# Scoring an attention in both orientations: keys on the partitions instead of transposed probabilities, in five attentions of a four-level decoder on one core

## What is computed

```python
s = q @ k.T * D ** -0.5          # 128 queries x nk keys
s = where(causal, s, -inf)       # L0_attn and L2_attn only
a = softmax(s, axis=-1)
o = a @ v
out = x + concat(o) @ Wo (+ bo)
```

## Time and profile before

| | |
|---|---|
| median of 3 runs | 4947.15 us (4937.4 to 4949.03) |
| profiled execution: span from its first to its last instruction | 4969.4 us |
| profiled execution: own time beside the span | none is given; the span stands 22.2 us above the median of the runs |
| PE busy | 4410.3 us, 89% |
| DVE busy | 2640.3 us, 53% |
| ACT busy | 2593.2 us, 52% |
| POOL busy | 836.2 us, 17% |
| mean granted TensorE clock | 0.958 |

### The profile page before, as it was taken

The page is one execution under the profiler, slowest core; times in us unless marked ns, Lnnn a source line. Parts: engine busy times, 40 slices in busy tenths (PEclk is TensorE's granted clock), DMA queues, the critical chain, the costliest instruction groups (busy, mean ns, idle before and its releaser), DMA issues.

```text
span 4969.4 us, 84778 instructions
## 1 busy us (share of the span) xinstructions
PE 4410.3 (89%) x29077; PEld 2535.4 (51%) x29077; DVE 2640.3 (53%) x6880; ACT 2593.2 (52%) x9813; POOL 836.2 (17%) x1454
## 2 busy tenths in 40 slices
PE   7888989989999999989799888998889888898796
PEld 3544764444454454448355444454455454554493
DVE  5555225655655655645454656556664565546523
ACT  4556434454454454453555556555655566555542
POOL 0111420011011011035021021110131021210350
PEclk9999989999999999999899989999999999999897
DMA  5000540000000000007000000000000000000172
GB/s 198 11 11 11 172 128 18 12 7 28 12 7 28 12 7 18 6 22 222 22 22 10 5 5 24 14 10 1 6 23 14 9 6 10 10 1 1 46 230 76
DMA packets 107750, 183.05 MB, mean 37 GB/s; under 512 B 13344, under 2 KB 69408, under 8 KB 107200
## 3 DMA queue, kind: packets, MB, share of 16 engines
q1 hardware_dynamic: 92544, 147.48, 9.9%
q0 software_dynamic: 13632, 28.04, 1.6%
q10 hardware_dynamic: 1152, 2.10, 0.1%
HBM read 126.33 MB, written 51.23 MB: 36 GB/s over the span
## 4 chain that ended last, share of the span: by engine, by line
PE 65%; DVE 20%; ACT 7%; issue 5%; DMA 2%; POOL 1%; SPq 0%; DVEq 0%; POOLq 0%; ACTq 0%
PE bank L713 8%; PE bank L866 7%; PE bank L883 6%; DVE rowmax L1693 6%; PE bank L745 4%; PE bank L1041 3%; PE bank L733 3%; PE bank L1152 3%; PE bank L1141 3%; PE bank L1023 3%; PE bank L790 3%; DVE probsT L1759 2%; PE bank L922 2%; PE bank L852 2%; ACT work L1323 2%
## 5 line engine op out<-in xcount | busy, mean ns | idle before, releaser
L1323 ACT ACTIVATE work<-bank,rowmax 128x128 f32<-128x128 f32 (+1 forms) x3072 | 1061.1, 398 | 208.6 <-DVE rowmax L1693 208.6
L1693 DVE TENSOR_REDUCE rowmax<-bank 128x4 f32<-128x512 f32 (+2 forms) x1152 | 614.0, 578 | 433.4 <-PE bank L866 314.8
L713 PE MATMUL bank<-mask_causal,identb 128*128 128x512 bf16 x2839 | 803.1, 394 | 22.6 <-DVE qd L1628 8.7
L883 PE MATMUL bank<-ident,work 128*128 128x128 f32 (+1 forms) x4096 | 641.0, 282 | 155.6 <-DVE probsT L1759 116.7
L1323 ACT ACTIVATION_READ_ACCUMULATOR work<-bank,rowmax 128x1 f32 x3072 | 753.1, 245 | 0.0
L883 PEld LDWEIGHTS bank<-ident,work 128*128 128x128 f32 (+1 forms) x4096 | 481.8, 144 | 377.7 <-DVE probsT L1759 196.8
L1759 DVE COPY probsT<-bank 128x512 f32<-128x512 f32 (+2 forms) x832 | 482.0, 601 | 55.3 <-PE bank L883 53.9
L713 PEld LDWEIGHTS bank<-mask_causal,identb 128*128 128x128 bf16 x2839 | 273.5, 101 | 290.7 <-issue 115.5
L866 PE MATMUL bank<-km,q 32*128 32x512 f32 (+2 forms) x1792 | 403.7, 562 | 1.9 <-issue 1.9
L2206 POOL TENSOR_TENSOR qd<-work 128x256 f32<-128x256 f32 (+1 forms) x64 | 64.7, 1012 | 1902.9 <-ACT work L1321 1836.5
L1257 ACT ACTIVATE part<-bank,eps 128x512 f32<-128x512 f32 x232 | 157.7, 680 | 383.8 <-PE bank L745 383.3
(11 more groups left out here) (336 smaller groups left out, 6902.5 us busy)
## 6 DMA issues: line engine op xcount, KB each, us to landing
slot<-in_w_L_ffn SPq DMA_DIRECT2D x78, 578.0 KB
slot<-in_w_stream SPq DMA_DIRECT2D x41, 512.0 KB
expert_rows<-slot SPq DMA_DIRECT2D x36, 516.0 KB, 6.3
slot<-in_w_L_ffn SPq DMA_DIRECT2D x39, 450.0 KB
qd<-expert_rows SPq DMA_DIRECT2D x117, 129.0 KB
back<-pair_rows SPq DMA_DIRECT2D x24, 512.0 KB, 5.3
slot<-in_w_stream SPq DMA_DIRECT2D x16, 256.0 KB
pair_rows<-qd,dest POOLq DMA_INDIRECT x234
```

The source lines that it names most:

```text
L713: nc.tensor.matmul(b[:], identb[:], mask["causal"][:].unsqueeze(1).to_broadcast([P, 4, P]), start=True, stop=True)
L883: ins = nc.tensor.transpose(b[0:nk, j * P:(j + 1) * P], probs[t % 2][:, r, j, 0:nk], ident[:])
L1323: ins = nc.scalar.activation(out, raw, ACT.Exp, bias=top, accum_out=expsum[t % 2][:, 4 * r + j:4 * r + j + 1])
L1693: V.tensor_reduce(m[:, 4 * r:4 * r + J], banks.where(("scores", n, c, s, r))[:, 0:J * nk] .rearrange("p (j k) -> p j k", j=J), AX_X, ALU.m ...
```

## The change

Five attentions get a body of their own, `keyed_mha`. The scores are made twice. The first time, with queries on the partitions, they only give the maxima. The second time, with the keys on the partitions (weights: the keys of one head; moving: its queries), they are what the exponential reads, so its result is already `probsT` and no transpose follows. Per item and engine:

- PE: `half(t, rows)` interleaves the score matmuls of two row groups of item t with the keyed ones of the two other row groups of item t-1, so that all four row tiles have work. Masked attentions add the mask to both, the second time with the mask as weights and the identity as moving operand. `turn_tops` turns the maxima (bf16, as value and remainder) with one matmul, `shift` adds them to the keyed scores with sixteen small bf16 matmuls (`top_pick`, 32 rows, as weights), `totals` makes the sums over the keys with sixteen matmuls on four column tiles, already spread over the features, `attend` and `output` are as before. The fillers in the body are gone but for six at t = 0 and four at t = 1.
- ACT: one copy of the turned maxima to bf16, four exponentials of 512 columns without bias and accumulator, Ln and Exp (scale -1) of the sums.
- DVE: the four maxima as before, two small instructions that split them in value and remainder (`split_tops`), `context`. No reciprocal, no copies out of PSUM.
- POOL: nothing (the halving sums of the three unmasked ones are gone).
- Rings: scores and turned maxima in banks 0 to 2, keyed scores and projections in 3 to 5, attend in 6, totals in 7.

Around it, `average64` gives way to a corner of `average` with a scale in the Ln, `after_mask` becomes bf16, `xcol` moves into `lcol`.

```diff
+KEYED = ("L0_attn", "L1_xattn", "L2_attn", "L2_a2", "L3_ffn",)
+FRONT_ROWS, BACK_ROWS = (0, 1), (2, 3)
...
-                             "head": (4, 5)})
+                             "head": (4, 5), "first": (0, 1, 2), "second": (3, 4, 5)})
...
+            return not st["linear"] and not st["mask"] and not keyed(st) and r in POOL_SUMS
...
+                    def half(t, rows):
+                        back = BACK_ROWS if rows == FRONT_ROWS else FRONT_ROWS
...
+                            for r in rows:
+                                b = bank(("scores", n, c, s, r), ("row_max", (n, c, s, r)), "first")
+                                if st["mask"]:
+                                    nc.tensor.matmul(b[:, 0:4 * nk], identb[:], mask[st["mask"]][:].unsqueeze(1)
+                                                     .to_broadcast([P, 4, P]), start=True, stop=False)
+                        if 1 <= t <= GROUP:
+                            c, s = items[t - 1]
+                            for r in back:
+                                b = bank(("keyed", n, c, s, r), ("probsT", (n, c, s, r)), "second")
+                                if st["mask"]:
+                                    nc.tensor.matmul(b[:], mask[st["mask"]][:], identb[:].unsqueeze(1)
+                                                     .to_broadcast([P, 4, P]), start=True, stop=False, skip_group_check=True)
+                        for j in range(4):
...
+                                    elif j == 0:
+                                        nc.tensor.matmul(b[:, 0:4 * nk], B["q"][c][g32, s * P:(s + 1) * P],
+                                                         km[c][g32, s, :, 0:nk], start=not st["mask"], stop=True
...
+                                    if D == 32:
+                                        keys, queries = k4[c][g32, j, s * nk:(s + 1) * nk], q4[c][g32, j, s * P:(s + 1) * P]
+                                    else:
+                                        keys, queries = km[c][g32, s, j, 0:nk], B["q"][c][g32, s * P:(s + 1) * P]
+                                    nc.tensor.matmul(banks.where(("keyed", n, c, s, r))[0:nk, j * P:(j + 1) * P], keys, queries,
+                                                     start=j == 0 and not st["mask"], stop=False, skip_group_check=True)
...
+                    def turn_tops(t):
...
+                        pe.wait_ge(*have("tops", (n, c, s)))
+                        nc.tensor.matmul(b[:, 0:P], tops[:], identb[:], start=True, stop=True
...
+                    def shift(t, rows):
...
+                        if rows == BACK_ROWS:
+                            pe.wait_ge(*have("tops_taken", (n, c, s)))
+                        for j in range(4):
+                            for r in rows:
+                                g32 = slice(32 * r, 32 * r + 32)
+                                ins = nc.tensor.matmul(banks.where(("keyed", n, c, s, r))[0:nk, j * P:(j + 1) * P],
+                                                       top_pick[g32, j:j + 1].to_broadcast([32, nk]), topsT[g32, :], start=False, stop=True,
+                                                       skip_group_check=True)
...
+                    def totals(t):
...
+                                if D == 32:
+                                    ins = nc.tensor.matmul(b[g32, j * P:(j + 1) * P], average[0:nk, 0:32], probsT[t % 2][0:nk, r, j, :],
+                                                           start=True, stop=True)
+                                else:
+                                    ins = nc.tensor.matmul(b[g32, 0:P], W("head_ones", nk)[:, 24 - 8 * j:56 - 8 * j],
+                                                           probsT[t % 2][0:nk, r, j, :], start=j == 0, stop=j == 3)
...
+                    for t in range(GROUP + 2):
+                        if t == GROUP + 1:
+                            step(then)
+                        if t == 0:
+                            warm(6, "second")
+                        half(t, FRONT_ROWS)
+                        if 1 <= t <= GROUP:
+                            turn_tops(t - 1)
+                        if t >= 2:
+                            totals(t - 2)
+                        elif t == 1:
+                            warm(4, "second")
+                        if 1 <= t <= GROUP:
+                            shift(t - 1, BACK_ROWS)
+                        half(t, BACK_ROWS)
+                        if 1 <= t <= GROUP:
+                            shift(t - 1, FRONT_ROWS)
...
+                        if t >= 2:
+                            attend(t - 2)
+                        if t == GROUP + 1:
+                            step(then)
+                        for c in C:
+                            if t == output_step(c):
+                                output(c)
...
+                    def soften(t):
...
+                        for r in BACK_ROWS + FRONT_ROWS:
+                            act.wait_ge(*have("keyed", (n, c, s, r)))
+                            nc.scalar.activation(probsT[t % 2][0:nk, r, :, :], banks.where(("keyed", n, c, s, r))[0:nk, :]
+                                                 .rearrange("p (j t) -> p j t", j=4),
+                                                 ACT.Exp).then_inc(*made("probsT", (n, c, s, r)))
+
+                    def invert(t):
...
+                        nc.scalar.activation(out, banks.where(("summed", n, c, s))[:, 0:w * P].rearrange("p (i t) -> p i t", i=w),
+                                             ACT.Ln, scale=float(P) if D == 32 else 1.0).then_inc(*made("log_sum", (n, c, s)))
+                        act.wait_ge(*have("log_sum", (n, c, s)))
+                        nc.scalar.activation(out, out, ACT.Exp, scale=-1.0).then_inc(*made("inverse", (n, c, s)))
```

239 lines of the change are left out of this document (231 added, 8 removed).

## The result

The forecast was wrong, in sign too. The changed kernel takes 5155.99 us (median of 4 runs, 5113.23 to 5178.47), the kernel before 4948.09 beside it (4 runs, 4937.4 to 4954.45): **1.0405 times as long, 95% interval 1.0346 to 1.0464**. Forecast were 4902 us and a range of 4850 to 4990. The profiled execution of the change took 5171.79 us with a span of 5170.1, which is 200.7 more than the span before.

The account below looks back on a forecast made before the run. PE was taken as the bound after the change, ACT's bound in masked items gone. Changes of -5.5, +1.6, -4.7, -1.7 and -1.0 us per body, four bodies each, gave -45 us from 4947: 4902 us, range 4850 to 4990.

Parts of the forecast that it names:

- The likeliest case: Whole kernel: new bodies save 45 us, 4902 us; with its better neighbour, the wait mostly covered (4855), chance 0.60.
- the clock: Rival: without fillers PE's granted clock drops, 7 us more low level in each of 20 bodies, 4972 us; chance 0.08.
- the forecast's own rule: Clock rival's pricing: half of the added low-level time is lost, +70 us over the 20 bodies.
- the forecast of -45: All five attentions, four bodies each: change against the kernel before, 45 us less.
- Items at 2.4 GHz: Time per item inside the bodies: masked 7.07, L3_ffn 5.79, 77 keys 5.85 us.
- last intervals: End of a body, up to the last attend: 2.5 us, 3.0 where a matmul centres the next norm.
- The wait for the exponential: Unmasked items' back half: PE waits for ACT to free a keyed bank, 0.95 us after the first shift.
- The passes do not queue up: Likeliest case: four tiles run at once, 1.08 us per half; opposite rival, queueing: +110 us, 5012, chance 0.12.
- the shift's weights are fast: Likeliest case: an item's two shifts cost 0.25 and 0.32 us; opposite rival, slow weights: +49 us, 4951, chance 0.20.
- The starts of bodies: Time to first attend: 16.0 us in L3_ffn, 14.3 L1_xattn, 23.0 L2_a2, 18.9 L2_attn, 22.6 L0_attn.
- The routing term: Masked bodies: routing matmuls of the group before add 1.2 us per body.
- the -11 of the masked bodies: Four bodies each of L0_attn and L2_attn: forecast change of -6.8 and -4.0 us.

Follow-up runs that it names:

- e14_first_item_fill: Change in three unmasked attentions only, banks recut, six fillers at each body's head and four at its first turn: 4867.31 us, 0.9824 of the kernel before.
- e11_rings_head_fill: Change in three unmasked attentions only, banks recut, six fillers at each body's head and two in each item: 4912.84 us, 0.9915 of the kernel before.
- e4_xattn_only: The change in L1_xattn alone, the other four attentions as in the kernel before: 5107.68 us, 1.0196 of the kernel before.

## Why the prediction was wrong

- **The likeliest case failed at one step: the clock, priced at 7 us of low level per body with a chance of 0.08.** The reason written against it was "a stall is under 1 us and followed by dense work". The stalls were of that size, 0.63 and 0.77 with one of 1.25. What failed is the second half: in bodies with 77 keys the dense work of the items did not bring the clock back in any of the 33 bodies that were low there, even with PE busy for 36 of 36 us. The low time was 294 us in four bodies of L1_xattn and 188 in four of L2_a2, 60 us per body and not 7. The mechanism was on the list; its size was off by a factor of over eight in these two kinds, and its chance was far too low. Over all twenty bodies the low time grew by 535 us and not by 140. By the forecast's own rule, that half of it is lost, that is an estimated 267 us, which covers the 246 between the forecast of -45 and the measured +201.
- **I took it as one price for all bodies.** L3_ffn has 128 keys and got 7 to 14 us of low level per body; there the clock does come back within the body, and the price of 7 was about right.
- **Items at 2.4 GHz were right.** Masked 7.05 (forecast 7.07), L3_ffn 5.85 (5.79), 77 keys 5.74 (5.85), last intervals 2.28 to 2.31 and 2.96 (2.5 and 3.0), end 2.9 (3.0). The wait for the exponential is there, 0.77 to 0.84 per unmasked item (0.95; the 0.69 in it came from a row of the norm's Ln, and the 512-wide exponentials, L1487, took 0.59 in the mean), ACT's busy time in an L0_attn body fell to 26.5 us (some 30), and the variance matmul waits for the square (34 times, 23.9 us in all). Bodies that kept the clock, with fillers in that wait: 57.8, 55.6, 70.6 against 57.3, 55.9, 71.0.
- **The passes do not queue up,** and the shift's weights are fast: with either rival the items would be 0.9 or 0.5 us longer. In an L3_ffn item of the changed kernel the keyed scores (L1037) start 0.01 behind the first long passes (L1026) and half a microsecond ahead of the second:

```profile
4831.70 0.70 PE L1026 MATMUL bank<-km,q 32*128 32x512 f32 x2 [0.84 <-ACT probsT L1487]
4831.71 0.71 PE L1037 MATMUL bank<-q,km 32*128 32x128 f32 x8
4832.20 0.62 PE L1026 MATMUL bank<-km,q 32*128 32x512 f32 x2
```

  In e14_first_item_fill the two shifts of a 77-key item, start to start of the next matmul, take 0.25 and 0.32.
- **The starts of bodies were too short in places.** First attend in L3_ffn 16.9 where the clock held (16.0), in L0_attn 23.5 to 23.9 (22.6), in L2_attn 19.2 (18.9), in L2_a2 23.8 (23.0).
- **The routing term was too small:** 1.2 us per body reckoned, 2 x 1.84 measured in six bodies, 22 us in all. I had counted the matmuls and not asked whose bank they take. 16.1 of the 22 are the waits for ACT's Ln. That, 24 us more of low level and the longer starts turn the -11 of the masked bodies into +21.
- **What would have shown it** was written down: "granted clock under 0.95 in the windows of the bodies". It was 0.52 to 0.64 in L1_xattn.

## What to carry to other kernels

Before a filler is removed, ask not how long the gap is that it leaves but whether the work behind it wins the clock back; where it doesn't, as in most of these bodies with 77 keys that fell, the price is half speed for most of the stage. Put such fillers where PE would otherwise wait at the head of a stage, a few and once, since they are cheap there (six and four of 0.22 us per body) and dear in every item (28 us in e11_rings_head_fill). When banks are dealt out anew, ask of every tenant, in every stage that it visits, whose reader it will wait for. When a change frees other engines but makes PE the bound, give the new waits a bank first; here that was worth 1.1 us per item (5.74 to 4.64).

## What the runs showed of the hardware

- The same instructions ran at either level for a whole body: L2_a2 in 70.6 or 107.3 us, L1_xattn in 48.4 or 77 to 82. In the traces with keyed bodies of 77 keys, with or without a wait in the items, the 24 bodies that fell within 5 us of their start spent 8 to 94 us at the low level, 19 of them over 50.
- Of 33 such bodies that were low in their items none came back there, and 24 came back 2 to 5 us after the output projection of chain 0 began.
- The fall depends on more than the program: with equal work in them, the four bodies of a kind differed inside one execution.
- Four tiles ran beside each other with passes of different length: in an L3_ffn item two of 512 columns on two row tiles and eight of 128 on the two others took 1.0 us (4831.70 to 4832.71), and the short ones began ahead of the second long ones (4832.20).
- The kernel before differed by 1.1 to 1.4% between chips (4948 to 4959 us, and 5015 to 5018). It has a trace on one chip alone; the same old masked bodies in e4_xattn_only take 318 and 317 us (L0_attn, L2_attn), where it has 296 and 292, which is 47 of the some 60 to 70 us.
